# Moving one half of a norm's transposes behind the slot's last score unit, in a one-core language model tower

## What is computed

```python
h = tok_ref(x, codebook, W1, b1, W2, b2)          # take rows, gelu MLP
h = h + attn_ref(layernorm(h), Wq, Wk, Wv, Wo, q_phase_angle, alibi_log_slopes)
h = h + ffn_ref(layernorm(h), U1, V1, c1, U2, V2, c2)
# attn: rotated q, scores + slope * (row - column), causal,
#       e / (1 + sum(e)), times v, times Wo
# ffn:  P = y @ U1;  H = gelu(P @ V1 + c1);  Q = H @ U2;  Q @ V2 + c2
```

## Time and profile before

| what | us |
|---|---|
| median of 3 runs (lowest, highest) | 953.24 (951.85, 954.5) |
| profiled execution, its own time | 954.45 |
| its span, first to last instruction | 952.6 |
| outside the span | 1.85 |

### The profile page before, as it was taken

The page is one execution under the profiler, slowest core; times in us unless marked ns, Lnnn a source line. Parts: engine busy times, 40 slices in busy tenths (PEclk is TensorE's granted clock), DMA queues, the critical chain, the costliest instruction groups (busy, mean ns, idle before and its releaser), DMA issues.

```text
span 952.6 us, 16893 instructions
## 1 busy us (share of the span) xinstructions
PE 865.0 (91%) x5552; PEld 670.9 (70%) x5552; DVE 607.5 (64%) x1898; ACT 728.7 (76%) x1611; POOL 629.7 (66%) x599
## 2 busy tenths in 40 slices
PE   7999668999999998999899999999999989999976
PEld 6888646767866786578667866787667866787663
DVE  4565636776685658575847684767676775668421
ACT  6855248998788868986889688977887798869813
POOL 6000068899686877687768877787859786768620
PEclk9999868999999999999999999999999999999997
DMA  9333350001000200020001100010001000000000
GB/s 268 63 111 111 126 184 1 1 2 56 2 1 1 78 1 1 1 79 1 1 1 45 35 1 1 23 57 1 1 23 56 2 1 23 1 2 1 10 14 22
DMA packets 23605, 33.55 MB, mean 35 GB/s; under 512 B 2608, under 2 KB 20176, under 8 KB 23520
## 3 DMA queue, kind: packets, MB, share of 16 engines
q1 hardware_dynamic: 19760, 19.01, 6.3%
q0 software_dynamic: 3760, 13.48, 5.0%
HBM read 17.80 MB, written 14.68 MB: 34 GB/s over the span
## 4 chain that ended last, share of the span: by engine, by line
PE 41%; DVE 13%; POOL 13%; ACT 10%; issue 10%; DMA 0%; DVEq 0%; POOLq 0%; ACTq 0%
PE ps L1039 11%; POOL probs L751 10%; PE ps L1173 9%; PE ps L1157 5%; DVE probs L921 5%; PE ps L1145 4%; PE ps L1125 4%; ACT probs L785 4%; PE ps L1146 3%; ACT turned_sb L792 3%; POOL token_rows L739 3%; DVE o_lo L973 2%; PE ps L1119 1%; ACT q_both L802 1%; DVE xn L910 1%
## 5 line engine op out<-in xcount | busy, mean ns | idle before, releaser
L751 POOL TENSOR_SCALAR probs<-probs,sums 128x512 f32<-128x512 f32 (+3 forms) x512 | 545.2, 1081 | 159.8 <-DVE sums L930 159.4
L921 DVE CUSTOM_DVE_ANT_0 probs<-ps,causal,slope 128x512 f32<-128x512 f32 (+3 forms) x512 | 260.2, 547 | 135.4 <-PE ps L1146 133.7
L785 ACT ACTIVATE probs<-probs,least 128x512 f32<-128x512 f32 (+3 forms) x512 | 284.4, 557 | 37.7 <-DVE least L921 31.1
L792 ACT ACTIVATE turned_sb<-ps 128x1280 f32<-128x1280 f32 x128 | 157.4, 1229 | 59.3 <-PE ps L1157 59.2
L1145 PE MATMUL ps<-k_hi,q_both 128*128 128x512 f32 (+3 forms) x512 | 183.1, 358 | 20.5 <-DVE least L921 18.3
L1157 PE MATMUL ps<-ident,probs 128*128 128x128 f32 x1280 | 162.0, 274 | 5.5 <-POOL probs L751 5.5
L1173 PE MATMUL ps<-turned_sb,token_rows 128*64 128x512 f32 (+3 forms) x1024 | 152.0, 438 | 13.4 <-ACT turned_sb L792 13.4
L1146 PE MATMUL ps<-k_lo,q_both 128*128 128x512 f32 (+3 forms) x512 | 153.4, 325 | 0.0
L1157 PEld LDWEIGHTS ps<-ident,probs 128*128 128x128 f32 x1280 | 143.6, 141 | 6.9 <-POOL probs L751 6.7
L1173 PEld LDWEIGHTS ps<-turned_sb,token_rows 128*64 128x64 f32 x1024 | 74.9, 136 | 98.7 <-issue 81.8
L1145 PEld LDWEIGHTS ps<-k_hi,q_both 128*128 128x128 f32 x512 | 97.1, 190 | 65.2 <-DVE least L921 39.3
(11 more groups left out here) (194 smaller groups left out, 1426.0 us busy)
## 6 DMA issues: line engine op xcount, KB each, us to landing
out_dram<-token_rows SPq DMA_DIRECT2D x7, 512.0 KB, 2.9
token_table<-made SPq DMA_DIRECT2D x4, 768.0 KB, 4.0
rows<-in_L_tok_codebook_dram SPq DMA_DIRECT2D x4, 512.0 KB, 9.0
w_f<-in_L_tok_W_dram SPq DMA_DIRECT2D x8, 256.0 KB, 6.3
early_rows<-made SPq DMA_DIRECT2D x4, 512.0 KB, 2.9
early_values<-xn SPq DMA_DIRECT2D x4, 512.0 KB, 3.0
token_table<-xn SPq DMA_DIRECT2D x4, 512.0 KB, 4.3
wo_f<-in_L_attn_Wo_dram POOLq DMA_DIRECT2D x1, 1024.0 KB, 9.8
```

The costliest lines, as they stand in the source:

```text
L751: ins = pool.tensor_scalar(at, at, recip[:, s % P_RING, q:q + 1], None, ALU.mult)
L785: act.activation(at, at, ACT.Exp, bias=least[:, s % P_RING, q:q + 1], scale=-1.0, accum_out=sums[:, s % P_RING, q:q + 1]).then_inc(exped, 1)
L792: act.activation(turned_sb[:, s % 2, :], turn_ps, ACT.Copy).then_inc(moved, 1)
L921: dve.tensor_tensor_reduce(out=probs[:, s % P_RING, at], in0=bank(unit % 2)[:, UNIT_AT[q]:UNIT_AT[q] + P * (q + 1)], in1=causal[:, at], sc ...
```

## The change

`("y", b, 0)` is taken out of `first(s)` and put into `second(s)`, ahead of `("y", b, 1)`. The slot stays the same.

```diff
@@ def first(s) @@
     if i + 1 < B and j == 7:
         out.append(("x", i + 1, 0))
-    if i >= 1 and j == 8 + LAG:
-        out.append(("y", i - 1, 0))
     if 1 <= i < B and j == 1 + LAG:
@@ def second(s) @@
         if j == 8 + LAG:
-            out.append(("y", b, 1))
+            out += [("y", b, 0), ("y", b, 1)]
         if j == 9 + LAG:
             out.append(("u", b, 0))
```

## The result

| what | us |
|---|---|
| kernel before, median of 5 runs | 953.69 |
| changed kernel, median of 5 runs (lowest, highest) | 958.52 (957.31, 959.03) |
| ratio, with its 95% interval | 1.0052 (1.004 to 1.0065) |
| the changed kernel again, beside other kernels: median, ratio | 957.03, 1.0032 (1.0021 to 1.0043) |
| profiled execution of the changed kernel, its own time and span | 958.72, 956.9 |

The change makes the kernel slower, by 4.8 us in the one measurement and by 2.8 in the other (957.03 against 954.20, the kernel before beside it). The forecast was 957.4 us, 4.2 more than before.

The account below looks back on a forecast made before the run. The prediction took TensorE, busy 91%, and in this stretch equally VectorE, as the bound. Seven passes times 0.60 us at `u` gave 4.2 us on the median 953.24, so 957.4 us, range 954.6 to 959.8.

Parts of the forecast that it names:

- Step 1: TensorE, slot 26: `values` no longer waits behind `xn`'s transposes and starts 1.3 us earlier, as does scores unit 2.
- Step 2: TensorE, slot 26: the first half's four transposes follow at about 272.5 without any wait, the same 0.63 us of work.
- Step 3: TensorE, slot 26: second half's transposes wait some 0.7 us for `a_bank`, held until VectorE's `q` low halves; worth 0.
- the 1.3 us: TensorE's gain at `values`, said to go into 0.3 us idle for `turned_sb`, 0.7 for the bank, rest first-half transposes.
- Step 4: VectorE, into slot 27: `invert` done some 0.7 us earlier, block four 0.3 earlier, but block one waits for TensorE; 0.
- Step 5: ScalarE: two high halves in a row make `turned_sb` 0.17 us later, covered ahead of slot 27's first `exps`; counted 0.
- Step 6: VectorE, slot 27: two low halves in place of one; `u`, released by the low half without slack, starts 0.60 us later.
- Step 7: Behind `u`: `rank_both` and all compute engines move by 0.60 us a pass; eighth sequence 0.
- the first: Rival: TensorE's seven 1.04 us waits for `xn` go and nothing replaces them, 7.3 us faster, 945.9 us; chance 0.05.
- The second rival: No change: the 0.7 us gap opening on VectorE pays for the second low half's 0.60, 953.2 us; chance 0.13.
- The third: Rival: ScalarE is the bound and its second high half adds 0.47 us a pass, 3.3 more, 960.7 us; chance 0.05.

Follow-up runs that it names:

- turn_first: Changed kernel with `turn` ahead of both halves' transposes in slot 26 on TensorE, filling the bank wait: 950.97 us, ratio 0.9977.
- only_low: Kernel before with only VectorE's part of the change, the first half's low half next to the second's in slot 27: 956.69 us, ratio 1.0035.
- low_back: Changed kernel with only VectorE's part undone, the first half's low half behind `o_rest` in slot 26 again: 952.99 us, ratio 0.9996.
- late_before: Kernel before with `u` waiting for the low halves only ahead of its last two products: 952.42 us, ratio 0.9985.
- both: turn_first's kernel with `u` also waiting for the low halves only ahead of its last two products: 950.43 us, ratio 0.9959.
- before_turn: Kernel before with `turn` ahead of the second half's transposes in slot 26, the first half where it was: 953.89 us, ratio 1.0002.

## Why the prediction was right

Step 1 held: `values` at 0.81 us after `xn`, 0.8 forecast. Step 2 held as well, with no wait ahead of the first half.

Step 3, the bank, is the one that turned an expected gain into nothing, and it held: the second half starts at 4.68, forecast 4.67 to 4.73. Its wait is told as 0.63 us where I had 0.7. Its account of where the 1.3 us go is wrong in one term: the 0.3 us of idle time for `turned_sb` lie ahead of `values` and are already taken off in the 1.3. The measured 1.27 split into 0.44 for the first half's transposes (their step, 273.76 to 274.20), about 0.8 of waiting and the 0.05 that are left. No term of the forecast's sum rests on this. turn_first is what shows that it was this wait that held the scores of slot 27, and not something else that happens to end at the same time.

Step 4 held: VectorE idle for 0.77 us ahead of block one, which stayed at 7.04 (forecast: about 0.6 to 0.7; block four came 0.38 us earlier, not 0.3). Step 5 held: `turned_sb` 0.10 us later, where I had 0.17, and covered. The cover is thin: in turn_first, where TensorE is earlier, the same two high halves make it wait 0.51 us for `turned_sb`.

Step 6, the second low half: 0.60 us forecast, 0.62 measured at `u`. only_low has it alone, and low_back, which undoes it alone, takes back 0.42 of the 0.62 (its high half is late). That `u` was held by the low half and not by `turn`, which I read from two equal lags of 0.14 us, is confirmed by late_before: without that wait `u` starts earlier. That it starts just 0.14 us earlier is chance: the lag is the time from the low half's end to `u`, and `turn` happened to be through as the low half ended.

Step 7 held: 0.62 at `u`, 0.62 at `rank_both`, 0.61 in the first pass and on the average of the six passes without the odd delay, though single passes have 0.48 to 0.89. The sum was 4.2, and 3.9 if the third pass lost its odd delay. It did, and the trace has 3.91. The medians say 4.8 and 2.8, on both sides of it. That the 957.4 lies so near to both medians is partly luck, since the clock of the last stretch alone moves an execution by more than that.

Of the rivals, the first (7.3 us faster) is excluded by the trace: the seven waits did go, and others took their place. The rule of the Trainium skill that I set beside it ("Perfetto Trace Analysis", section "Optimization Strategy": find the gaps of the engine, find what they wait for, make it start sooner or finish faster) leads to this gap; the runs show that emptying it was worth nothing until the next wait of the same engine was filled too. The second rival (no change) described what would happen without the bank, and turn_first bears it out in part: with block one 0.84 us earlier, two low halves in slot 27 cost less than what was won. The third (ScalarE) did not come true for this change: the first `exps` stayed at 7.84. ScalarE's two high halves become a bound one step on, in both, by way of `turn` and not of `exps`.

## What to carry to other kernels

When work is taken out of an engine's wait, follow the engine to its next wait before counting the gain: here a bank that another engine still had to read took the 1.27 us back at the third step behind it, and other work put into that second gap brought 0.84 of it out. And when one list sets the order of several engines, cost the move on each of them: the whole price of this change was one instruction of 0.60 us that changed places on VectorE, from a spot with slack to one that `u` waited for. Where two waits end within 0.1 us of each other (`u` could start at 9.07 for the one and at 9.14 for the other), taking away either looks worthless and only both together pay, here 0.7 us a pass.

## What the runs showed that I had not expected

The third pass of the kernel before has its fourth block 0.35 us late with no wait in the program to explain it. It is no chance: the traces of only_low, before_turn and late_before, all made from the kernel before, have it in the same pass at the same place (5.39 or 5.40 after `xn` in place of 5.04), and none of the traces made from the changed kernel has it in any pass. TensorE is not late there. The last score matmul that this block needs ends 4.89 us after `xn` in the third pass (`xn` at 467.94) as in the second (the same matmul at 373.07, `xn` at 368.46):

```profile
472.55 0.28 PE L1146 MATMUL ps<-k_lo,q_both 128*128 128x256 f32 x1
```

So the 0.35 us lie between that end and VectorE's start, and the gap that the earlier trace rows puts down to `ps` is not all TensorE's. The cause stays open; the delay goes with the program, not with the execution. In only_low VectorE's gap swallows it, as the prediction had supposed.

The median of the kernel before moved by up to 0.7 us from one set of runs to the next (953.54, 953.89, 954.20), and the changed kernel's two ratios differ by 0.2%. For a change of 0.4% the positions within a pass, which repeat to 0.03 us, told more than the times. The last stretch is a second thing that I had not counted on: its length moves with the granted clock by 2.8 us from trace to trace, two thirds of the change's whole effect.
